# Attention scores on one core: four heads in full-height products of nine parts, rewritten as two heads on each of the two 64-row sides of TensorE with six parts and a separate mask product

## The reference

```python
attn = jnp.einsum('bhqd,bhkd->bhqk', q, k) / jnp.sqrt(jnp.asarray(hd, x.dtype))
alibi = -slopes[None, :, None, None] * (Tt - 1 - jnp.arange(Tt))[None, None, None, :]
attn = attn + alibi
attn = jnp.where(causal, attn, jnp.finfo(x.dtype).min)
p = jax.nn.softmax(attn, axis=-1)
out = jnp.einsum('bhqk,bhkd->bqhd', p, v).reshape(Bb, Tt, C)
return out @ Wo + bo
```

## Time and profile before

| | us |
|---|---|
| median of 3 runs | 1278.57 |
| lowest, highest | 1277.38, 1294.37 |
| span of the profiled execution (the page gives no other time for it) | 1285.2 |
| attention stage in that span | 280 to 943 |
| steps 2 and 3 of it, from one "out" to the next | 31.7 and 31.0 |

### The profile page before, as it was taken

One profiled execution on the slowest core, in us unless ns is written; L12 is line 12 of the kernel. 1 busy time (PEld: TensorE's weight loads), 2 busy tenths in 40 slices (PEclk: granted clock), 3 DMA queues, 4 the chain that ended last, 5 costly groups with the idle time before them and its releaser, 6 DMA issues. The chain is left out here.

```text
span 1285.2 us, 20321 instructions
## 1 busy us (share of the span) xinstructions
PE 1010.8 (79%) x6768; PEld 603.9 (47%) x6768; DVE 804.3 (63%) x2127; ACT 546.7 (43%) x878; POOL 487.5 (38%) x484
## 2 busy tenths in 40 slices
PE   5872119952589999999899998898888989998882
PEld 3661017741134434444335443343257868884551
DVE  4667860132686888788987888768627533555654
ACT  1431004422126656656566654464563433432141
POOL 3101145525504610352016420232434444556776
PEclk9885558985559999999999998887899999999995
DMA  4225403421321311131122232153137755642122
GB/s 115 66 66 166 73 11 95 120 64 36 106 75 32 110 43 44 35 107 41 41 67 88 88 84 66 42 156 120 46 89 213 209 159 158 175 129 58 46 76 64
DMA packets 113122, 114.88 MB, mean 89 GB/s; under 512 B 17813, under 2 KB 95253, under 8 KB 109781
## 3 DMA queue, kind: packets, MB, share of 16 engines
q1 hardware_dynamic: 73830, 74.07, 20.9%
q0 software_dynamic: 12048, 25.71, 7.2%
q10 hardware_dynamic: 27144, 13.83, 3.7%
HBM read 67.94 MB, written 41.94 MB: 85 GB/s over the span
## 5 line engine op out<-in xcount | busy, mean ns | idle before, releaser
L2159 DVE TENSOR_REDUCE maxima<-psum 128x1 f32<-128x512 f32 (+4 forms) x624 | 384.6, 642 | 106.1 <-PE psum L1974 54.9
L2097 ACT ACTIVATE probs<-psum 128x1024 f32<-128x1024 f32 (+3 forms) x384 | 299.0, 809 | 262.6 <-PE psum L1993 199.3
L2007 PE MATMUL psum<-probs,v_wide 128*32 128x512 f32 (+3 forms) x1536 | 173.7, 526 | 0.0
L1970 PE MATMUL psum<-ka,qa 75*128 75x512 bf16 (+3 forms) x440 | 146.6, 345 | 22.6 <-DVE maxima L2159 16.6
L1481 POOL DMA_INDIRECT sorted<-x_rows,to_row x76 | 75.4, 992 | 213.4 <-ACT probs L2097 118.4
L2518 ACT ACTIVATE g_silu<-psum 128x512 f32<-128x512 f32 x80 | 47.8, 597 | 177.1 <-PE psum L2424 105.0
L1989 PE MATMUL psum<-qa,ka 78*128 78x512 bf16 (+3 forms) x440 | 117.2, 332 | 4.7 <-DMA qa<-max_parts 2.4
L1407 POOL DMA_INDIRECT w_gu<-expert_out,to_row x64 | 65.8, 1029 | 137.0 <-ACT probs L2097 95.7
L2424 PE MATMUL psum<-w_gu,g_xT 128*128 x384 | 97.1, 396 | 9.1 <-DVE g_h L2594 5.5
L1970 PEld LDWEIGHTS psum<-ka,qa 75*128 75x128 bf16 x440 | 42.8, 99 | 123.8 <-DVE maxima L2159 104.0
L116 POOL DMA_INDIRECT f_got<-expert_out,dense x64 | 64.1, 1002 | 64.6 <-DMA f_got<-expert_out,dense 44.1
(11 more groups left out here) (333 smaller groups left out, 1823.3 us busy)
## 6 DMA issues: line engine op xcount, KB each, us to landing
g_rows<-sorted SPq DMA_DIRECT2D x192, 64.0 KB
expert_out<-g_y ACTq DMA_DIRECT2D x48, 256.0 KB, 2.8
qa<-q_steps SPq DMA_DIRECT2D x30, 192.0 KB
ka<-k_steps SPq DMA_DIRECT2D x10, 576.0 KB
w<-in_W SPq DMA_DIRECT2D x16, 256.0 KB, 3.0
w_gu<-in_gu SPq DMA_DIRECT2D x4, 1024.0 KB, 10.4
sorted<-blank SPq DMA_DIRECT2D x54, 64.0 KB
q_steps<-w_gu SPq DMA_DIRECT2D x12, 256.0 KB
```

Source lines behind the costliest of these rows:

```text
L1970: mm = pe.matmul(bank[:, h * width:h * width + plain], qa[b][0:ROWS_MAX, h0 + h, qt * P:(qt + 1) * P], ka[b][0:ROWS_MAX, h0 + h, seg * HAL ...
L2007: mm = pe.matmul(B[OUT][32 * h:32 * (h + 1), q0 - c * HALF:HALF], v_wide[s.buf][:, j, h, PAD * (1 - c):PAD * (1 - c) + 32], probs[k % PRIN ...
L2097: act.activation(probs[k % PRING][:, 2 * pair:2 * pair + 2, 0:w], PS[:, 2 * pair:2 * pair + 2, 0:w], ACT.Exp).then_inc(exps, 1)
L2159: dve.tensor_reduce(maxima[:, seg, h0:h0 + heads, qt], bank[:, 0:heads * width].rearrange("p (h k) -> p h k", h=heads), AX.X, ALU.max).the ...
```

## The change

Heads 0 and 1 of a group move to rows 0 to 63 of the operands, heads 2 and 3 to rows 64 to 127 (a *side* each). Of the nine products of parts the six largest stay: 48 rows, 51 with the distance term, 54 with the maximum. The mask rows leave the operands; a product of 43 rows from a small tile `mask` now goes into the bank first, and one product over the full width is added to it. A pair of heads in a slot is now one head of each side. Maxima units are made within a side and alternate between the sides; the unit of four heads by 128 columns becomes two units, so a step has 40. The operand sets shrink to half their columns and leave the room of `w_down`. A load is 14 DMAs of fewer bytes instead of 6.

```diff
-PROD = 3 * 3 * HD
+SIDES, PER_SIDE = 2, GH // 2
+SIDE = P // SIDES
+PRODUCTS = ((0, 0), (0, 1), (0, 2), (1, 0), (1, 1), (2, 0))
+PROD = len(PRODUCTS) * HD
 ALIBI_AT, MAX_AT = PROD, PROD + 3
 ROWS_MAX, ROWS_ALL = PROD + 3, PROD + 6
 MASK_GROUP = 3
-MASK_ROWS = -(-P // MASK_GROUP) // 16 * 16 + 16
-ROWS_DIAGONAL = ROWS_ALL + MASK_ROWS
+MASK_ROWS = -(-P // MASK_GROUP)
...
-            heads = max(1, min(GH, HALF // width))
-            if qt == 0:
-                heads = 2
-            units += [(qt, seg, h, heads, width) for h in range(0, GH, heads)]
+            heads = min(PER_SIDE, HALF // width)
+            units += [(qt, seg, side * PER_SIDE + h, heads, width)
+                      for h in range(0, PER_SIDE, heads) for side in range(SIDES)]
...
+def score_bank(h):
+
+    return h % PER_SIDE * SIDES + h // PER_SIDE
+
+
+def side_of(h):
+
+    return h // PER_SIDE * SIDE
...
 def emit_load(sp, G, I, s):
...
-    for j in range(3):
-        sp.dma_start(G.qa[s.buf][j * HD * 3:(j + 1) * HD * 3].rearrange("r h n -> r (h n)"),
-                     q.rearrange("o i (d h) n -> (o d) i (h n)", d=HD)).then_inc(G.here[s.buf], 16)
-    sp.dma_start(G.ka[s.buf][0:PROD].rearrange("r h n -> r (h n)"),
-                 k.rearrange("o j (d h) n -> (o j d) (h n)", d=HD)[:, None, :].to_broadcast([3 * HD, 3, GH * SEQ])
-                 ).then_inc(G.here[s.buf], 16)
+    q = G.q_steps[s.n:s.n + 1].rearrange("o j (u d p) n -> u j (o d) (p n)", u=SIDES, d=HD)
+    k = G.k_steps[s.n:s.n + 1].rearrange("o j (u d p) n -> u j (o d) (p n)", u=SIDES, d=HD)
+    wide = [PER_SIDE * SEQ]
+    for side in range(SIDES):
+        at = side * SIDE
+        for part, first, copies in ((0, 0, 3), (1, 3, 2), (2, 5, 1)):
+            rows = slice(at + first * HD, at + (first + copies) * HD)
+            sp.dma_start(G.qa[s.buf][rows].rearrange("r h n -> r (h n)"),
+                         q[side, part][None, :, :].to_broadcast([copies, HD] + wide)).then_inc(G.here[s.buf], 16)
+            sp.dma_start(G.ka[s.buf][rows].rearrange("r h n -> r (h n)"), k[side, 0:copies]).then_inc(G.here[s.buf], 16)
...
 def emit_load_direct(sp, G, Q, which, part):
-    heads = Q.parts[which][0:GH * HD, part, :]
-    rows = (G.qa, G.ka)[which][0]
-    for copy in range(3):
-        first = (copy * 3 * HD + part) if which == 0 else (part * 3 * HD + copy)
-        sp.dma_start(rows[first:first + 3 * HD - 2:3], heads).then_inc(G.here[0], 16)
+    for side in range(SIDES):
+        heads = Q.parts[which][side * SIDES * HD:(side + 1) * SIDES * HD, part, :]
+        for block, parts in enumerate(PRODUCTS):
+            if parts[which] == part:
+                at = side * SIDE + block * HD
+                sp.dma_start((G.qa, G.ka)[which][0][at:at + HD], heads).then_inc(G.here[0], 16)
...
+                        at = side_of(h0)
                         diagonal = seg * HALF + width == (qt + 1) * P
-                        plain = width - P if diagonal else width
                         for h in range(heads):
-                            if plain:
-                                mm = pe.matmul(bank[:, h * width:h * width + plain], qa[b][0:ROWS_MAX, h0 + h, qt * P:(qt + 1) * P],
-                                               ka[b][0:ROWS_MAX, h0 + h, seg * HALF:seg * HALF + plain],
-                                               start=(h == 0), stop=True, skip_group_check=True)
                             if diagonal:
-                                mm = pe.matmul(bank[:, h * width + plain:(h + 1) * width],
-                                               qa[b][0:ROWS_DIAGONAL, h0 + h, qt * P:(qt + 1) * P],
-                                               ka[b][0:ROWS_DIAGONAL, h0 + h, qt * P:(qt + 1) * P],
-                                               start=(h == 0 and plain == 0), stop=True, skip_group_check=True)
+                                pe.matmul(bank[:, (h + 1) * width - P:(h + 1) * width], G.mask[at:at + MASK_ROWS, 0, :],
+                                          G.mask[at:at + MASK_ROWS, 1, :], start=(h == 0), stop=False, skip_group_check=True)
+                            mm = pe.matmul(bank[:, h * width:(h + 1) * width],
+                                           qa[b][at:at + ROWS_MAX, (h0 + h) % PER_SIDE, qt * P:(qt + 1) * P],
+                                           ka[b][at:at + ROWS_MAX, (h0 + h) % PER_SIDE, seg * HALF:seg * HALF + width],
+                                           start=(h == 0 and not diagonal), stop=True, skip_group_check=True)
                     mm.then_inc(small, 1)
 
                 def emit_scores(s, k, pair):
...
                     q0 = max(c * HALF, j * P)
                     if k or s.n:
                         pe.wait_ge(exps, s.n * (2 * SLOTS) + 2 * k + pair - 1)
-                    for h in (2 * pair, 2 * pair + 1):
-                        out = B[h][:, 0:(c + 1) * HALF - q0]
-                        plain = q0 + P if q0 == j * P else q0
-                        if plain < (c + 1) * HALF:
-                            mm = pe.matmul(out[:, plain - q0:], ka[s.buf][0:ROWS_ALL, h, j * P:(j + 1) * P],
-                                           qa[s.buf][0:ROWS_ALL, h, plain:(c + 1) * HALF], start=True, stop=True,
-                                           skip_group_check=True)
-                        if plain > q0:
-                            mm = pe.matmul(out[:, 0:P], ka[s.buf][0:ROWS_DIAGONAL, h, j * P:(j + 1) * P],
-                                           qa[s.buf][0:ROWS_DIAGONAL, h, q0:plain], start=(plain == (c + 1) * HALF), stop=True,
-                                           skip_group_check=True)
+                    diagonal = q0 == j * P
+                    heads = (pair, pair + PER_SIDE)
+                    if diagonal:
+                        for h in heads:
+                            at = side_of(h)
+                            pe.matmul(B[score_bank(h)][:, 0:P], G.mask[at:at + MASK_ROWS, 1, :], G.mask[at:at + MASK_ROWS, 0, :],
+                                      start=True, stop=False, skip_group_check=True)
+                    for h in heads:
+                        at = side_of(h)
+                        mm = pe.matmul(B[score_bank(h)][:, 0:(c + 1) * HALF - q0],
+                                       ka[s.buf][at:at + ROWS_ALL, h % PER_SIDE, j * P:(j + 1) * P],
+                                       qa[s.buf][at:at + ROWS_ALL, h % PER_SIDE, q0:(c + 1) * HALF],
+                                       start=not diagonal, stop=True, skip_group_check=True)
...
-            in_room = [G.w_down[:, u * GH * SEQ // 2:(u + 1) * GH * SEQ // 2].bitcast(bf16).rearrange("p (h n) -> p h n", h=GH)
-                       for u in range(2)]
-            G.qa = [in_room[0] if b == EARLIEST_FREE else A.sb(f"qa{b}", [P, GH, SEQ], bf16) for b in range(BUFS)]
-            G.ka = [in_room[1] if b == EARLIEST_FREE else A.sb(f"ka{b}", [P, GH, SEQ], bf16) for b in range(BUFS)]
+            G.qa, G.ka = [[A.sb(f"{x}a{b}", [P, PER_SIDE, SEQ], bf16) for b in range(BUFS)] for x in "qk"]
+            G.mask = A.sb("mask", [P, 2, P], bf16)
```

More of the change, by code:

```diff
@@ L1038, in next, with loads_until @@
         return Step(self.n + by, b % BUFS, self.used + b // BUFS)
-LOADS = 6 * 16
+LOADS = SIDES * (2 * 3 + 1) * 16
+DIRECT_LOADS = SIDES * 2 * len(PRODUCTS)
+def loads_until(s):
+    return s.used * LOADS + LOADS + ((DIRECT_LOADS - SIDES * 2 * 3) * 16 if s.buf == 0 else 0)
 def emit_load_alibi(sp, G, I, s):
-    sp.dma_start(G.ka[s.buf][ALIBI_AT:ALIBI_AT + 6].rearrange("r h n -> r (h n)"), I["c_alibi"][s.n, 0:6, :]).then_inc(G.here[s.buf], 16)
-    sp.dma_start(G.qa[s.buf][MAX_AT:MAX_AT + 3].rearrange("r h n -> r (h n)"), I["c_alibi"][s.n, 6:9, :]).then_inc(G.here[s.buf], 16)
+    for side in range(SIDES):
+        at = side * SIDE + ALIBI_AT
+        sp.dma_start(G.ka[s.buf][at:at + 3].rearrange("r h n -> r (h n)"), I["c_alibi"][s.n, side]).then_inc(G.here[s.buf], 16)
@@ L1064, in emit_fixed_rows @@
 def emit_fixed_rows(sp, G, I):
     for b in range(BUFS):
[L1067 to L1070, removed]
+        for operand, first in ((G.qa[b], ALIBI_AT), (G.ka[b], MAX_AT)):
+            for side in range(SIDES):
+                at = side * SIDE + first
+                sp.dma_start(operand[at:at + 3].rearrange("r h n -> r (h n)"), I["c_ones"]).then_inc(G.ones_here, 16)
@@ L1071, in emit_fixed_rows @@
+    for which in range(2):
+        for side in range(SIDES):
+            sp.dma_start(G.mask[side * SIDE:side * SIDE + MASK_ROWS, which, :], I["c_mask"][which]).then_inc(G.mask_rows_here, 16)
     for n in range(2):
         emit_load_alibi(sp, G, I, Step(n, n, 0))
[L1075 to L1081, removed]
 def emit_load_direct(sp, G, Q, which, part):
-    heads = Q.parts[which][0:GH * HD, part, :]
-    rows = (G.qa, G.ka)[which][0]
-    for copy in range(3):
-        first = (copy * 3 * HD + part) if which == 0 else (part * 3 * HD + copy)
-        sp.dma_start(rows[first:first + 3 * HD - 2:3], heads).then_inc(G.here[0], 16)
```

(13 more changed lines are left out.)

17 lines of the change are left out of this document (5 added, 12 removed).

## The result

The changed kernel takes **1332.96 us** (median of 4 runs, 1330.04 to 1341.25) beside 1286.47 of the kernel before: ratio 1.0367, 95% interval 1.0294 to 1.0440. It is slower by 2.9 to 4.4%. The forecast was 1287 in 1250 to 1318, so the time lies outside the range, on the side of rivals 1 and 2. The forecast's +8 was counted from 1278.6, the median of three runs of the kernel before; with a fourth run that median is 1286.5, and +46 stands where +8 was forecast.

What follows compares the result with a forecast made beforehand. Neither PE nor DVE alone was taken to bound the attention step; they hand two banks to and fro. Terms +7 + 4 - 4 + 2 - 1 + 0 = +8 on 1278.6 gave 1287 us, range 1250 to 1318.

Steps and rivals of the forecast that it cites:

- rival 1: Attention stage: the two sides don't run side by side, second product 0.2 us behind the first; 1315 us, chance 0.13.
- rival 2: Attention steps: PE idles more behind the maxima and the clock falls in ten more steps; 1320 us, chance 0.10.
- Pairs: Score pairs: both products run side by side, 0.22 us instead of 0.43; PE freed of 3.0 us a step.
- DVE is the wall: Four-unit slots: PE's freed 0.4 us turns into waiting for DVE, above 82.7 us over the same 350 us.
- Rival 3: Attention units: DVE's reads are not the wall, two of PE's 3.0 freed us arrive; 1250 us, chance 0.17.
- The walk: Slot-by-slot timing of PE and DVE in a full step: +0.5 us a step, +7 over 14 steps.
- borders: Changes between half-height and full-height products: 0 to 0.15 us each, taken as 0.07, +4 us over the stage.
- The lower clock: Stretch from 780 to 930 us, partly at 1.2 GHz: pairs save more than masks cost, -4 us.
- First units: Start of the stage at low clock: some 40 masks lengthen the units' bank loop, +2 us.
- Last step: Final attention step: it has no units and ACT keeps its work, -1 us.
- Loads: Operand loads for step 0 and each step: more issues, fewer bytes; -2 to +3 us, taken as 0.
- PE's busy time falls by 20 us: Attention stage: sign that PE's busy time would fall by some 20 us and more.

Runs made afterwards that it cites:

- e6: Kernel before with unit and pair products cut to their first 64 rows, softmax left out; 1424.1 us, ratio 1.107.
- e7: Kernel before with unit and pair products cut to their first 66 rows, softmax left out; 1365 to 1423 us.
- e9: Changed kernel with operands padded by zero rows (units read 61 rows, pairs and masks 64); 1298.1 us, ratio 1.007 to the kernel before.
- e11: Kernel before with all unit and pair products reading 126 rows, softmax left out; 1271.1 us, ratio 0.984.
- e4: Changed kernel with six useless 512-column products per step in PE's wait for the maxima; 1330.7 us, ratio 1.032 to the kernel before.
- e2: Changed kernel with both heads of a pair taken from one side, so their products run in sequence; 1333.1 us, ratio 1.035 to the kernel before.
- e12: Kernel before with a second, zero-filled copy of the keys, so most off-diagonal products read 126 rows, result kept; 1275.2 us, ratio 0.993.
- e3: Changed kernel with maxima units and their masks reading both sides' rows, softmax left out; 1307.0 us, ratio 1.020 to the kernel before.
- e1: Changed kernel with every score pair and its masks computed twice; 1317.9 us, ratio 1.022 to the kernel before.

## Why the prediction was wrong

**The step that failed** is the chance of rival 2, 0.10, and under it the sentence "it held for 400 us in the same kind of slots". In the sum the clock stands only with -4, for the stretch from 780 to 930; that steps 1 to 10 could lose it is put at nothing. Six of them lost it for 10 to 34 us each and hold 33 of the stage's 38 us, and the sign named for rival 2, a PEclk that is not full from 380 to 780, came. The slots were of the same kind in time, but not in rows: their products read 75, 78 or 126 rows, the new ones 51, 54 or 43, and a unit that waits for DVE runs alone on its side (511.85, 512.45). I had counted PE's work as columns streamed, where rows are free, and only asked how long PE would idle. e6, e7, e9 and e11 show that the number of rows moves the clock, while steps at the same full clock keep their length.

Rival 2's size was near: 1320 against 1333, from 100 us more at 1.2 GHz where 127.6 came, at a third of a us each. Measured by the stage, one such us cost: changed against before 38.4 / 127.6 = 0.30, e9 against changed 32.1 / 115 = 0.28, e6 138 / 363 = 0.38, e11 16.4 / 45.5 = 0.36. Its mechanism (idle time behind "maxima") is at most a part: fillers in that wait brought back some of the clock and no time (e4), and rows of zeros, which leave the wait as it is, brought back 32 of the stage's 38 us (e9). So rival 2 was near in size for a reason that it did not name.

Point by point:

- *Pairs* run side by side, 0.01 us apart where both sides are free: rival 1 (0.13) is out. Its sign, a second product 0.2 behind the first, appears where a unit holds one side (500.13), and means there that unit and pair overlap. e2 shows that undoing it brings nothing.
- *DVE is the wall*: waits for it rose from 82.7 to 117.8 (125.2 in e9, at nearly the clock of before). Rival 3 (0.17) is out. The Trainium skill, "TensorEngine Tiling (Array Packing)", section PSUM Bottleneck, says that tiling speeds up TensorE but not the evacuation of PSUM; the 82.7 and 117.8 agree.
- *The walk*: slot 8 3.14 (said: 3.2), slot 3 1.82 (1.75). A step at full clock was to grow by 0.5, and by 0.3 for borders; the four that are at full clock in both kernels grew by 0.6 on average (-0.1 to 1.4). Mechanism and mean size hold; the upper end for borders, 0.6 a step, would have made 1.1. Which step grows by how much the walk does not say, and that is no scatter: steps 3 to 5 agree to 0.1 between before, e11 and e12, and between the changed kernel and e9.
- *The lower clock* (-4): the steps that were low before, 11 to 14, are 2.1 us longer, not shorter. Their low time rose from 56 to 82 us, so whether pairs and masks save there what was said is not shown.
- *First units* (+2): the first units and step 0 took 2.9 more. *Last step* (-1): -1.9.
- *Loads* (0, -2 to +3): from ACT's first `ka` issue to the first unit 16.5 before (319.98 to 336.47), now 18.5 (322.77 to 341.30). In the other traces it is 14.2 to 17.9 with nine `ka` loads and 16.8 to 19.1 with twelve, so about +2 belongs to the loads, inside the bounds. The rest of the 5.1 lies ahead of that issue, whose place differs by 4.9 us between runs of the kernel before and its variants alone. The first unit starts 4.8 us later, which by the prediction's last sentence would prove the walk wrong; it does not, as more than half of it lies ahead of the loads. Issues and first unit after:

```profile
322.77 5.16 ACTq L1103 DMA_DIRECT2D ka<-w_gu  x6
...
341.30 0.30 PE L1982 MATMUL psum<-mask 43*128 43x128 bf16 x2 [6.96 <-DMA ka<-w_gu]
```

- *PE's busy time falls by 20 us*: at full clock it falls by 1.7 in step 3; over the stage it rose from 550 to 568, since every product at 1.2 GHz is longer. A busy sum over two clocks says nothing about work.

What stays open: whether rows of the units, of the pairs or of the masks count most (all were padded together; e3 gave rows to the units and their masks alone, e1 to the pairs and theirs, and either brought the low time down, to 70 and 110), what besides rows moves the clock (e4, and e6 beside the changed kernel), and the price of a border between half-height and full-height products.

## What to carry to other kernels

Before products are split onto parts of the rows or thinned in rows, look whether the granted clock has reserve: here the kernel before held it for 400 us at 75 to 126 rows and lost it again and again at 64 and 66. In the changed kernel the clock took 32 us of the stage (changed less e9), all else 6 (e9 less before). Rows of zeros were a nearly free way to get it back: they gave 35 us in the changed kernel and some 9 in the one before, and steps 3 to 5, at full clock, did not grow by them. And a forecast of a stage should be made once per clock level, with the steps near the edge as a rival of full weight.

## What the runs showed that was not expected

- The granted clock goes with the rows that products read: 465, 397, 101 and 56 us at 1.2 GHz for 64, 66, 75 to 126, and 126 rows in one and the same program. Rows of zeros count too: 229 without them, 114 with them (e9). The Trainium skill, "TensorE: Matmul & The Clock Gate", section What's actually happening, says that the level depends on how busy PE has been. These runs agree only if busy is more than time: in e6, 88.70 us with PE busy for 88.54 stayed at 1.2 GHz.
- With fewer rows the low level also lasts longer. Its longest stretch inside steps 1 to 15 was 7 us in e11, 17 in the kernel before, 31 in the changed kernel, 89 in e6 (one execution each; e2 and e4, close to the changed kernel in rows, have 41 and 48).
